# Mean squares from a scaled Square and a constant column, and another place for layer 0's softmax normalisation

## The reference

```python
q = rms_norm(einsum('btd,ndh->btnh', x, q_kernel), q_norm_scale)     # 16 heads of 128
k = rms_norm(kv[0], k_norm_scale)                                    # 8 key heads, 8 value heads
# rms_norm: x * rsqrt(mean(square(x)) + 1e-6) * scale
q, k = apply_rope(q), apply_rope(k)     # concat([x1*cos - x2*sin, x2*cos + x1*sin])
logits = q . k * 0.0884, masked to the last 128 positions
probs = softmax(logits); enc = probs . v; x = x + enc . out_kernel
```

## Time and profile before

| | |
|---|---|
| median of the runs | 730.21 us (729.7 to 730.29, three runs) |
| the profiled execution: its own time | 729.91 us |
| the profiled execution: its span | 728.1 us |
| busy: PE, PEld | 703.5 us (97%), 628.1 us (86%) |
| busy: DVE, ACT, POOL | 494.2, 403.7, 359.4 us |
| granted TensorE clock | 1.0 of full speed |

### The profile page before, as it was taken

How to read it: one execution, slowest core, us unless ns; L and a number is a source line. 1 busy time by engine, 2 the same in 40 slices (tenths; PEclk the granted TensorE clock), 3 DMA queues, 4 the chain that set the end, 5 groups by cost and what they waited for, 6 DMA issues and landing times.

```text
span 728.1 us, 14855 instructions
## 1 busy us (share of the span) xinstructions
PE 703.5 (97%) x4296; PEld 628.1 (86%) x4296; DVE 494.2 (68%) x1698; ACT 403.7 (55%) x1205; POOL 359.4 (49%) x508
## 2 busy tenths in 40 slices
PE   4799999999999998999999999999999999989998
PEld 3589999999999987888889999999999999868887
DVE  6998888888888899769756554444444445567443
ACT  4576666666676663523256555555555555554221
POOL 3898888888887884002069532323232325317000
PEclk9999999999999999999999999999999999999999
DMA  6010110101020021100011010100101100000000
GB/s 230 2 44 2 44 46 1 43 0 43 0 101 29 0 87 73 45 1 0 16 59 59 3 57 17 43 27 32 43 15 56 45 0 14 2 13 1 1 30 29
DMA packets 9002, 24.64 MB, mean 34 GB/s; under 512 B 896, under 2 KB 3072, under 8 KB 8832
## 3 DMA queue, kind: packets, MB, share of 16 engines
q1 hardware_dynamic: 8240, 22.55, 8.9%
q10 hardware_dynamic: 720, 1.57, 0.6%
HBM read 23.07 MB, written 1.05 MB: 33 GB/s over the span
## 4 chain that ended last, share of the span: by engine, by line
PE 92%; DVE 4%; issue 1%; POOL 1%; DMA 0%; ACT 0%; DVEq 0%; POOLq 0%; ACTq 0%
PE bank L625 12%; PE bank L310 12%; PE bank L329 12%; PE bank L304 11%; PE bank L361 8%; PE bank L281 7%; PE bank L341 6%; PE bank L350 5%; PE bank L363 4%; PE bank L280 4%; PE bank L664 3%; PE bank L372 3%; PE bank L668 2%; DVE probs L449 1%; PE bank L684 1%
## 5 line engine op out<-in xcount | busy, mean ns | idle before, releaser
L437 ACT ACTIVATE probs<-scores,negmax 128x128 f32<-128x128 f32 (+1 forms) x256 | 115.6, 452 | 41.6 <-DVE negmax L485 40.9
L466 DVE TENSOR_TENSOR enc_lo<-bank,enc_hi 128x256 fp32r<-128x256 f32 x128 | 54.2, 424 | 118.0 <-PE bank L281 111.7
L385 ACT COPY probs_t<-bank 128x384 f32<-128x384 f32 x128 | 61.1, 478 | 121.1 <-PE bank L350 121.1
L529 POOL TENSOR_TENSOR a_hi<-raw_a,zero 128x384 fp32r<-128x384 f32 (+2 forms) x69 | 53.2, 771 | 104.9 <-PE bank L341 104.0
L449 DVE TENSOR_SCALAR probs<-probs,rinv 128x128 f32<-128x128 f32 (+1 forms) x256 | 85.1, 374 | 4.5
L361 PE MATMUL bank<-probs_t,v 128*128 128x256 f32 x256 | 77.1, 383 | 5.1 <-DVE enc_lo L466 4.8
L281 PE MATMUL bank<-qk 128*128 128x256 f32 x256 | 76.5, 380 | 0.0
L542 POOL TENSOR_TENSOR rms_r<-meansq,neg_half 128x3 f32<-128x3 f32 x64 | 58.2, 910 | 34.9 <-DVE meansq L519 34.7
L329 PE MATMUL bank<-b_hi,enc_hi 128*128 128x256 f32 x256 | 74.7, 292 | 0.0
L329 PE MATMUL bank<-b_lo,enc_hi 128*128 128x256 f32 x256 | 72.3, 282 | 0.0
L329 PE MATMUL bank<-b_hi,enc_lo 128*128 128x256 f32 x256 | 72.3, 282 | 0.0
(11 more groups left out here) (124 smaller groups left out, 2033.4 us busy)
## 6 DMA issues: line engine op xcount, KB each, us to landing
raw_a<-in_wa SPq DMA_DIRECT2D x10, 768.0 KB, 4.3
raw_a<-in_wa SPq DMA_DIRECT2D x9, 512.0 KB, 4.1
raw_b<-in_wb SPq DMA_DIRECT2D x16, 256.0 KB, 2.6
x<-in_x SPq DMA_DIRECT2D x4, 256.0 KB, 5.9
w_a<-in_w2t SPq DMA_DIRECT2D x1, 1024.0 KB, 4.8
raw_a<-in_wax SPq DMA_DIRECT2D x2, 512.0 KB, 3.5
raw_b<-in_wdown SPq DMA_DIRECT2D x2, 512.0 KB, 3.8
raw_a<-in_wa ACTq DMA_DIRECT2D x1, 512.0 KB, 4.5
```

The source lines that it names most:

```text
L437: nc.scalar.activation(probs[:, c % 4, c0:c1], scores[:, c % 2, c0:c1], ACT.Exp, bias=negmax[:, c % 2, r:r + 1], scale=-1.0, accum_out=row ...
```

## The change

The squares of layer 0 get a constant column. `squares` becomes three blocks of 129 columns, of which the last of each is set once to the epsilon; ScalarE squares the projection with a scale of 128^-0.5, so that a sum over 129 columns is the mean square plus epsilon. VectorE's own instruction for that (the old L519) is gone, and the sum is written to `meansq` directly. In layer 0 the normalisation no longer opens a slot with unit c - 1; it stands between the cosine and the sine product and serves unit c. In layer 1, and in layer 0 from slot 61 on, it stays.

```diff
-        sumsq = sb("sumsq", [P, 2, 3])
         meansq = sb("meansq", [P, 2, 3])
...
-        squares = gate[:, 0, 0:384]
+        squares = gate[:, 0, 0:3 * (DH + 1)].rearrange("p (a d) -> p a d", a=3)
...
-                    need(act, s["ss"], it, m)
-                    nc.scalar.activation(squares, bank[PJ_BANK + m % 2][:, 0:384], ACT.Square).then_inc(s["sq"], 1)
+                    if it is None and m == 0:
+                        act.wait_ge(s_eps, 1)
+                    need(act, s["ms"], it, m)
+                    nc.scalar.activation(squares[:, :, 0:DH], bank[PJ_BANK + m % 2][:, 0:384].rearrange("p (a d) -> p a d", a=3),
+                                         ACT.Square, scale=float(DH) ** -0.5).then_inc(s["sq"], 1)
...
             if c < TAIL_SLOT:
-                dve_normalise(dve, L, it, c)
+                if L == 1:
+                    dve_normalise(dve, L, it, c)
                 dve_residual(dve, L, it, c)
...
                 dve_maxima(dve, L, it, c)
-                dve_normalise(dve, L, it, c)
+                if L == 1 or c > TAIL_SLOT:
+                    dve_normalise(dve, L, it, c)
...
-                    nc.vector.reduce_sum(sumsq[:, m % 2, :], squares.rearrange("p (a d) -> p a d", a=3),
-                                         AX_X).then_inc(s["ss"], 1)
+                    need(dve, s["rp"], it, m - 1)
+                    nc.vector.reduce_sum(meansq[:, m % 2, :], squares, AX_X).then_inc(s["ms"], 1)
...
-                    need(dve, s["ss"], it, m + 1)
-                    need(dve, s["rp"], it, m - 1)
-                    nc.vector.tensor_scalar(meansq[:, m % 2, :], sumsq[:, m % 2, :], 1.0 / DH, RMS_EPS,
-                                            ALU.mult, ALU.add).then_inc(s["ms"], 1)
+
+                    dve_normalise(dve, L, it, c + 1)
                     need(dve, s["radd"], it, m - 1)
...
             nc.gpsimd.memset(neg_half[:, :], -0.5).then_inc(s_half, 1)
+            nc.gpsimd.memset(squares[:, :, DH:DH + 1], RMS_EPS).then_inc(s_eps, 1)
```

More of the change, by code:

```diff
@@ L152, in build @@
         s_scl, s_w2 = sem("scales_loaded"), sem("w2_loaded")
-        s_zero, s_half, s_scq = (sem(n) for n in ("zero_set", "half_set", "qscale_made"))
+        s_zero, s_half, s_eps, s_scq = (sem(n) for n in ("zero_set", "half_set", "epsilon_set", "qscale_made"))
         s_sin, s_cos, s_second = (sem(n) for n in ("sin_made", "cos_made", "second_head_tables"))
@@ L156, in build @@
         names = ("scores", "max", "exp", "rinv", "pnorm", "pt", "ptev", "pv", "ehi", "elo", "op", "opadd",
-                 "proj", "vproj", "qkev", "vev", "sq", "ss", "ms", "rp", "rot", "radd", "roped", "tq", "tqev",
+                 "proj", "vproj", "qkev", "vev", "sq", "ms", "rp", "rot", "radd", "roped", "tq", "tqev",
                  "a0hi", "a0", "ahi", "a", "bhi", "b")
```

## The result

The changed kernel takes 731.49 us (median of 19 runs), the kernel before 730.29 us in the same comparison (19 runs). The ratio is 1.0016, 95% interval 1.0009 to 1.0022: it is slower by 1.2 us, between 0.7 and 1.6 us. The forecast of 730.5 us was 0.3 us above its own base of 730.21. The time lies 0.1 us inside the wide range (728.9 to 731.6) and 0.1 us outside the forecast's own range (729.9 to 731.4). A loss of 1.2 us ahead of slot 0, for which the forecast had no term, met a gain of 0.9 us in the tail that it had not expected. The profiled spans are 729.5 us after and 728.1 us before.

What follows compares the result with a forecast made beforehand. TensorE (PE) was taken to bound the kernel, 92% of the chain. Start -0.13, short slots +0.45 and tail 0 summed to +0.3 us on 730.21, giving 730.5 us; own range 729.9 to 731.4, wide range 728.9 to 731.6.

Steps and rivals of the forecast that it cites:

- The loop costs 0: Slots 6 to 59: PE bounds them; `rot_b` ends at S + 3.15, its room shrinks from 0.98 to 0.39 us, cost 0.
- POOL's A split misses the normalisation by 0.03 us: Loop, behind an A split: POOL ends 3.02 us behind `rot_b`'s end, the next normalisation comes at 3.05 us.
- slower, by POOL's A split: Rival, loop: the A split overruns the normalisation's new place, which waits; +1.4 to +10 us, chance 0.12 for over +1.5.
- The two held multiplications go: Start: POOL's L544 can't run before `rot_b`, so two normalisation multiplications are no longer held: -0.56 and -0.82 us.
- L1246 is held, +0.90: Start: POOL's L544 holds VectorE's weight split L1246; bounds 0 and +0.90 us, taken as +0.90.
- the split isn't held: Rival, start: L1246 runs on beside POOL, 0.90 us less than forecast, 729.6 us; chance 0.25.
- Race with `b_lo`, +0.20: Start: unit 2's normalisation starts close to POOL's `b_lo`; 0 to +0.46 us, taken as +0.2.
- the rival of an untouched start (0): Rival, start: the change does nothing there, since another wait, a tile's layer norm, ends last; 730.2 us, chance 0.1.
- `rms_r` starts earlier: Start: POOL's `rms_r` no longer waits for the cosine product, 0.54 us earlier; bounds 0 and -0.54, taken as -0.30.
- `meansq` goes ... cost 0: Loop: dropping VectorE's 0.07 us `meansq` instruction, with 54 of 64 slots in PE's shadow, costs 0.
- Short slots, 3 times 0.15: Slots 3 to 5: projection 0.33 us late, between 0 and +1.0 in all; part absorbed, 0.15 each taken, +0.45 us.
- The tail, 0 with -0.5 as its end: Tail: POOL's back-to-back weight splits bind VectorE, so 0 is taken; bounds -0.5 and +0.2 us.

Runs made afterwards that it cites:

- the move from slot 3 on: Both repairs, but the normalisation is moved from slot 3 on instead of from slot 6 on, against the kernel before: 729.86 us, 0.9989.
- both repairs: Changed kernel, `rms_r` waiting for the cosine product in units 0 to 3, normalisation moved only from slot 6; against the kernel before 728.92 us (0.9980), again 728.65 (0.9974).
- the mean squares' part alone: Kernel before plus scaled square, epsilon column and one sum without the `meansq` instruction; normalisation at its old place: 735.58 us, 1.0071 against the kernel before.

## Why the prediction was right, and where only by luck

- *The loop costs 0*: right for the whole change. 203.34 and 203.33 us; room of `rot_b` as forecast (end at S + 3.15); idle time ahead of L468 0.58 on average (28.6 us over 49).
- *POOL's A split misses the normalisation by 0.03 us*: right, it misses by 0.01, and `rms_r` holds nothing (the multiplications of the changed kernel's loop take at most 0.35 us, as in the earlier trace rows). The rival "slower, by POOL's A split" falls.
- *The two held multiplications go*: right (28.95 and 33.04, 0.55 us for each pair). *L1246 is held, +0.90*: mechanism right, size 0.71 (L1249 took 1.12 us against 0.41). The rival "the split isn't held" falls. *Race with `b_lo`, +0.20*: 0.21 (0.76 for the pair at 36.10). From the first scores to the projection that these terms lead up to pass 10.33 us (27.14 to 37.47), before 10.43 (25.48 to 35.91): -0.10, the forecast had -0.13. By this sum alone the rival of an untouched start (0) would be as near; it falls because the parts moved as forecast.
- *`rms_r` starts earlier, "I take -0.30"*: this step failed; taken as a whole, the earlier `rms_r` has the other sign. The forecast looked for what waits for `rms_r` and saw only a gain. It did not ask what POOL does next: the rotation sum behind it starts 0.25 to 0.70 us earlier, measured against VectorE's rows, and meets VectorE's layer-norm multiplications in the three slots ahead of slot 0. The forecast had used this very hold for the normalisation and for the weight split, and had not carried it to L233, so the stretch ahead of slot 0 had no term at all. Cost 1.22 to 1.47 us in the four kernels with the early `rms_r` (12.31 to 12.56, against 10.97 to 11.10 in the other nine profiles). In the changed kernel 0.43 us of it come at a granted clock of 1.00; how much of the other 0.79 is held time and how much the lower clock was not separated. Between slots 0 and 8 the mean squares' part does pay, 0.34 to 0.46 us, where the forecast had 0.51 (0.21 and 0.30).
- *"`meansq` goes ... cost 0"* in the loop held only because the normalisation moved as well. Taken alone the part costs 4.84 us there. The forecast summed the two parts as if they were independent.
- *Short slots, 3 times 0.15*: mechanism right, size wrong. Two projections came late and not three, by 0.38 and 0.49 us where the forecast had 0.33 and took 0.15; with the move from slot 3 on the loss is 0.98 us, the upper bound. No run shows that a part of the delay is absorbed, and held multiplications ahead of `rot_b` added to it.
- *The tail, 0 with -0.5 as its end*: wrong; -0.92, beyond the bound, and "a tail that is shorter" was one of the forecast's own signs of being wrong. The forecast expected the splits to decide whatever the phase. The holds still exist (1.49 and 1.04 us, as forecast), but add up to less; that this is the gain is not shown.
- *The sum*: forecast +0.3, measured +1.2, or +0.93 by the stretches. From the forecast's 0.32 to these 0.93 lead +1.22 ahead of slot 0, +0.32 between slots 0 and 8 (0.64 instead of 0.32) and -0.92 in the tail. The number was near by luck: two errors upwards met one downwards.

## What to carry to other kernels

When an instruction leaves the path of another engine, ask what that engine starts next, when, and which instruction runs beside it then: here the part of the change that removes a 0.07 us instruction cost 5 us by itself, and a wait put back for four units gained 1.3 us. Test the parts of a change apart and together, since one part may cover what the other breaks. Cut the profile at a few marks: most stretches repeat within 0.04 us between kernels that do the same there, where the whole time scatters by 1 us. Not all do: ahead of slot 0 the changed kernel took 12.31 us and three others with the same order there 12.56.

## What the runs showed of the hardware

- A POOL instruction that streams many columns (here 128 to 512) holds a VectorE `tensor_scalar` from SBUF to SBUF until it ends (layer-norm 0.98 us instead of 0.40, softmax 1.06 instead of 0.29), and a `tensor_tensor` with both inputs in SBUF (1.12 instead of 0.41). POOL's `rms_r` (0.86 us, 128x3) holds neither: the multiplications that start inside it take at most 0.35 us, and in the kernel before L1246 starts at 28.05, inside the `rms_r` of 27.42 to 28.28, and takes its usual 0.41 us. A subtraction with one input in PSUM takes its usual 0.42 us inside the rotation sum (L468 at 154.26, L546 from 153.44 to 154.45). The Trainium skill, "SBUF — State Buffer", section "Who interferes with whom", says that the shared port pair is locked for a whole instruction; the traces agree for the streaming ones and not for `rms_r`.
- PE's granted clock fell to 0.57 on average between 24 and 28 us, so in part to the lower of its two levels, in the changed kernel (0.50 from 25 to 27 us), and to 0.64 to 0.70 in the three others with an early `rms_r`. PE had idled 1.86 to 1.89 us in these four ahead of the projection of tile 4 (22.89 in the changed kernel). In the other nine profiles the idle time at that place was 1.30 to 1.37 us, and the clock stayed at 1.00. No run changed this idle time by itself.
- The first twelve matmuls of the projections start 0.43 us apart and take 0.63 us each (the first 0.77) until they drop to 0.39. In the kernel before they do so from the tenth on (12.74), in one profile of both repairs not at all. The granted clock reads 1.00 there, so it doesn't explain this; in the mean squares' part alone matmuls of the same form take 0.63 us from 23 to 24 us at a granted clock of 0.50. The first mark came at 15.73 and 14.38 us in two profiles of the same kernel (both repairs). Behind the FFN's start, three profiles (both repairs twice, and from slot 3) were 0.7 us shorter than the others (440.6 against 441.3 us), with no change there; its cause stays open.
